# Mixture-of-experts stage: the order of 16 tiles of 512 rows and 7 of 256

## The chip, the cores and the metric

The kernel runs on one core of a Trainium2 chip. The core has five engines that run side by side, each with its own instruction stream: TensorE (PE, matmuls), VectorE (DVE), ScalarE (ACT), GpSimd (POOL) and SyncE (SP, which here only starts DMAs). They wait for each other through semaphores. The metric is the device time of one execution in microseconds; lower is better.

## What is computed

One decoder layer on x of shape 16 x 256 x 256 in float32: linear attention with decay, cross attention to a short context, and a mixture of 8 experts of which each token uses two, each stage followed by a residual and a layer norm. Only the last part matters here:

```python
probs = softmax(xf @ router_w.T); topv, topi = top_k(probs, 2)
mask = zeros.at[arange(n)[:, None], topi].set(1.0)
probs = probs * mask / (sum(probs * mask) + 1e-09)
g = einsum('nd,edf->nef', xf, gate_w) + gate_b     # d = 256, f = 512
u = einsum('nd,edf->nef', xf, up_w) + up_b
h = silu(g) * u
expert_out = einsum('nef,efd->ned', h, down_w) + down_b
y = einsum('ne,ned->nd', probs, expert_out)
x = layernorm(x + y)
```

4096 tokens with two experts each give 8192 rows of work.

## The kernel before

**Stages.** `linear_attention`, `cross_attention`, `route_tokens`, `run_experts` and `combine` run one after the other. The expert stage runs from about 1046 us to 1442 us of the span.

**Tiles.** `Plan` cuts the expert work into tiles. A tile belongs to one expert. There are BIGS = 16 tiles of T = 512 rows (four blocks of 128) and HALVES = 7 of HALF = 256 rows (two blocks), enough for every split of the rows over the experts. The big tiles are numbered 0 to 15 and the half ones 16 to 22. `blocks(t)` gives a tile's blocks and `first_block(t)` where its rows stand in the table of slots; `blocks_of_parity(t, turn)` and `rounds(t)` count blocks for the semaphores. `route_tokens` finds each row's slot and writes in `expert_of` and `tile_table` which expert each tile has.

**One tile.** Products of float32 are made from a high and a low part: hi x hi + hi x lo + lo x hi. In its turn for tile t each engine does the following, in the order of its code.

- PE: gate and up for f = 0, 1 (`gate_up`, L2095), the down product of tile t-1 block by block (`down`, L2107), the transposes of the rows of tile t+1 (`turn_x`, L2084), and gate and up for f = 2, 3. A big tile has 48 gate/up matmuls of 512 columns, a half one 48 of 256; a down has 12 matmuls of 256 columns per block. Two blocks of `down` fit in PSUM; the third waits until DVE has taken the first (`y_kept`).
- ACT: the high part of the gate/up weights of t+1 (`gu_high`, L1895), silu of gate 0 and 1 (L1917), the scaling of the y rows of t-1 by the router's share (L1927) between the high parts of h (L1923), the high part of the rows of t+1 (L1907), gates 2 and 3, and the high part of the down weights of t+1 (L1901).
- DVE: h for f = 0, 1 (L2023), then `keep_y` of t-1: a cast of the row numbers (`e_target<-e_token`, L1987, one column for each block) and one addition for each block that takes it out of PSUM (L1991). Then the low part of the rows of t+1 (L1980), the shares of t+1 (L2004), the row numbers to gather for t+2 (`e_index`, L2013), h and its low parts (L2029), and the low part of the down weights (L1996).
- POOL: the low part of the gate/up weights of t+1 (`low_parts`, L1862, four subtractions), `add_rows` of t-1 (L1873, one indirect DMA for each block that adds y rows to `sum_rows`), and `gather_rows` of t+2 (L1853, one indirect DMA for each block). The addition waits until ACT has scaled the rows (`y_scaled`).
- SP: the weights of t+2 (L1808 for gate and up, L1812 for down), 1.5 MB for a tile of either size, and the biases of t+1 after the y rows of t-1 are kept.

All buffers that depend on a tile are double, by the parity of t. `all_tiles` writes out tiles 0 and 1, runs tiles 2 to 13 in a hardware loop of two tiles an iteration, and writes out tiles 14 to 22.

## Time and profile before

| | |
|---|---|
| median of 3 runs | 1469.36 us (1468.21 to 1469.93) |
| the profiled execution | 1471.37 us, of it the span 1469.7 us |
| mean granted TensorE clock | 0.949 of full |
| busy: PE, PEld, DVE, ACT, POOL | 90%, 76%, 55%, 65%, 54% |
| six tiles 9 to 14 | 106.4 us |
| tile 15 | 23.1 us |
| tiles 16 to 21 | 76.9 us |
| tile 22, to the end of its tail | 14.4 us |

A tile is counted here from its first gate/up matmul. PE is TensorE's matmuls and PEld its weight loads, which overlap. In a timeline a row gives start, length, engine, line, operation, what is written and read, shapes and a count of merged instructions; brackets hold the idle time before it and what ended it. PEclk is the share of the full TensorE clock of 2.4 GHz that was granted, so 0.50 is 1.2 GHz. Matmuls overlap, so the length of one is more than the distance to the next.

### The profile page before, as it was taken

To read this page: it belongs to the slowest core of one execution; us is meant where nothing else is said; L and a number is where in the kernel's file an instruction comes from. 1 tells how busy PE (TensorE), PEld (TensorE's weight loads), DVE (VectorE), ACT (ScalarE), POOL (GpSimd) and SP (SyncE) were. 2 spreads that over 40 slices of the span, in tenths; PEclk is the share of its full clock that TensorE was granted. 3 is DMA by queue.
4 is the path that set the end of the run, shared out by engine and by line. 5 is a ranking of instruction groups with operands and counts; after the bars stand their busy time and mean duration, and the time that the engine had idled before them with its cause. 6 is when DMAs were issued, how large, how long until landed. Compare 5 with 4: busy or idle time off the path is not lost. (4 is left out here: it accounts for less than half of the span.)

```text
span 1469.7 us, 31082 instructions
## 1 busy us (share of the span) xinstructions
PE 1322.1 (90%) x10437; PEld 1120.0 (76%) x10437; DVE 811.3 (55%) x1684; ACT 953.2 (65%) x2168; POOL 796.1 (54%) x885
## 2 busy tenths in 40 slices
PE   5899999999999999999987999973599999998780
PEld 4788888888888888888775777752488888888780
DVE  4345554455554455554556888848355555555464
ACT  4677777777777777777754777763455655665453
POOL 2244444444444444444555777740468888886863
PEclk9999999999999999999998999985699999999895
DMA  3300100000000010000023444323346666665637
GB/s 136 81 11 27 31 23 30 16 28 25 30 23 30 15 30 24 31 30 23 23 65 91 113 111 111 98 74 92 105 109 151 154 151 154 168 156 122 193 77 236
DMA packets 136852, 117.55 MB, mean 80 GB/s; under 512 B 46578, under 2 KB 121690, under 8 KB 136730
## 3 DMA queue, kind: packets, MB, share of 16 engines
q1 hardware_dynamic: 121754, 95.36, 21.4%
q0 software_dynamic: 14976, 20.62, 7.8%
q8 instruction: 70, 1.15, 0.3%
q14 instruction: 52, 0.43, 0.1%
HBM read 79.89 MB, written 33.58 MB: 77 GB/s over the span
## 5 line engine op out<-in xcount | busy, mean ns | idle before, releaser
L345 POOL TENSOR_SCALAR_AFFINE_SELECT a_decay<-a_decay 128x256 f32<-128x256 f32 x256 | 115.2, 454 | 258.3 <-ACT a_decay L433 256.8
L565 DVE TENSOR_TENSOR a_probs<-a_ps_s,a_decay 128x384 f32<-128x384 f32 x256 | 131.6, 552 | 158.6 <-PE a_ps_o L752 147.5
L354 POOL TENSOR_TENSOR a_key_sum<-a_probs 128x256 f32<-128x256 f32 x128 | 94.5, 738 | 169.9 <-DVE a_probs L565 157.9
L396 ACT ACTIVATE a_qk_exp<-a_ps_qk 128x512 f32<-128x512 f32 x128 | 76.5, 598 | 137.5 <-PE a_ps_qk L658 130.0
L1873 POOL DMA_INDIRECT sum_rows<-e_y_out,e_target x78 | 124.4, 1594 | 48.2 <-ACT e_y_out L1927 21.1
L658 PE MATMUL a_ps_qk<-a_xT_hi,a_w_hi 128*128 128x256 f32 x512 | 144.8, 283 | 3.6 <-ACT a_qk_relu L397 3.6
L658 PE MATMUL a_ps_qk<-a_xT_hi,a_w_lo 128*128 128x256 f32 x512 | 143.9, 281 | 0.0
L658 PE MATMUL a_ps_qk<-a_xT_lo,a_w_hi 128*128 128x256 f32 x512 | 143.7, 281 | 0.0
L558 DVE SCALAR_TENSOR_TENSOR a_qk<-a_qk_exp,a_qk_relu 128x512 f32<-128x512 f32 x128 | 89.1, 696 | 94.5 <-ACT a_qk_relu L397 94.3
L733 PE MATMUL a_ps_s<-a_qk 64*128 64x256 f32 (+1 forms) x1024 | 132.2, 338 | 0.7 <-DVE a_probs L565 0.5
L431 ACT ACTIVATE a_decay<-a_ps_c,a_c_now 128x256 f32<-128x256 f32 x256 | 124.4, 486 | 2.0 <-PE a_ps_c L723 1.2
L1853 POOL DMA_INDIRECT e_x_in<-x_rows,e_index x78 | 78.6, 1007 | 75.4 <-DVE e_index L2013 52.2
L1862 POOL TENSOR_TENSOR e_gu_lo<-e_gu_raw,e_gu_hi 128x512 fp32r<-128x512 f32 x88 | 110.4, 1290 | 8.9 <-ACT e_gu_hi L1895 8.5
L746 PE MATMUL a_ps_o<-a_probs,a_values 128*64 128x256 f32 (+1 forms) x1024 | 111.5, 338 | 0.4 <-DVE a_probs L565 0.4
L733 PEld LDWEIGHTS a_ps_s<-a_qk 64*128 64x128 f32 x1024 | 107.8, 187 | 2.5 <-issue 2.5
L658 PEld LDWEIGHTS a_ps_qk<-a_xT_hi,a_w_hi 128*128 128x128 f32 x512 | 97.8, 191 | 5.7 <-issue 5.6
L2107 PE MATMUL e_ps_y<-e_dn_hi,e_hid_hi 128*128 128x256 f32 x312 | 91.0, 292 | 9.4 <-DVE e_y_out L1991 7.3
L433 ACT ACTIVATE a_decay<-a_ps_c,a_c_now 128x128 f32<-128x128 f32 x256 | 98.4, 385 | 0.0
L658 PEld LDWEIGHTS a_ps_qk<-a_xT_hi,a_w_lo 128*128 128x128 f32 x512 | 98.0, 191 | 0.0
L658 PEld LDWEIGHTS a_ps_qk<-a_xT_lo,a_w_hi 128*128 128x128 f32 x512 | 97.8, 191 | 0.0
L359 POOL TENSOR_TENSOR a_oT_lo<-a_oT,a_oT_hi 128x256 fp32r<-128x256 f32 x128 | 94.3, 737 | 1.2 <-ACT a_oT_hi L450 1.2
L1033 POOL TENSOR_TENSOR b_probs<-b_probs,b_top 128x1232 f32<-128x1232 f32 x32 | 72.8, 2274 | 40.8 <-DVE b_top L1228 40.8
(317 smaller groups left out, 4008.1 us busy)
## 6 DMA issues: line engine op xcount, KB each, us to landing
e_gu_raw<-in_L_ffn_gate_w SPq DMA_DIRECT2D x23, 512.0 KB
e_gu_raw<-in_L_ffn_up_w SPq DMA_DIRECT2D x23, 512.0 KB
e_dn_raw<-in_L_ffn_down_w SPq DMA_DIRECT2D x23, 512.0 KB
a_x_in<-in_x SPq DMA_DIRECT2D x16, 256.0 KB, 2.7
a_x_res<-in_x SPq DMA_DIRECT2D x16, 256.0 KB
x_rows<-a_x SPq DMA_DIRECT2D x16, 256.0 KB, 2.2
x_bo_rows<-a_x_bo SPq DMA_DIRECT2D x16, 256.0 KB, 2.2
b_x_bo<-x_bo_rows SPq DMA_DIRECT2D x16, 256.0 KB, 2.8
```

The lines of the kernel that those rows point to most:

```text
L345: pool.affine_select(out=d, in_=d, compare_op=ALU.is_ge, fill=0.0, base=0, pattern=[[0, 2], [1, P]], channel_multiplier=-1)\
L354: pool.tensor_tensor(key_sum[:], probs[:, :, P:N], probs[:, :, N:TRI], ALU.add).then_inc(keys_summed, 1)
L359: pool.tensor_tensor(oT_lo[g % 2][:], oT[g % 2][:], oT_hi[g % 2][:].bitcast(F32), ALU.subtract).then_inc(oT_lo_done, 1)
L431: act.activation(decay[h][:, 0:N], ps_c[:, h, :], ACT.Exp, bias=c_now[:, 0, head:head + 1], scale=-1.0)
L433: act.activation(decay[h][:, N:TRI], ps_c[:, h, P:N], ACT.Exp, bias=c_now[:, 1, head:head + 1], scale=-1.0).then_inc(decay_exp[h], 1)
L565: vec.tensor_tensor(probs[:, h, :], ps_s[h][:, 0:TRI], decay[h][:], ALU.mult)\
L658: mm = pe.matmul(out, l, r, start=(n == 0), stop=(n == len(todo) - 1))
L733: mm = pe.matmul(ps_s[h][:, out], qk[g][rows, 1, j], qk[g][rows, 0, i], start=True, stop=True)
L746: pe.matmul(out[h][:, 0, cols], values[par][:, j, 2 * g + h, :], probs[:, h, keys], start=(j == 0), stop=(j == 1), skip_group_check=True)
L1862: ins = pool.tensor_tensor(gu_lo[par][:, k, cols], gu_raw[par][:, k, cols], gu_hi[par][:, k, cols].bitcast(F32), ALU.subtract)
L1873: pool.indirect_dma_start(sum_dram, bass.IndirectOffsetOnAxis(target[par][:, blk:blk + 1], 0), y_out[par][:, blk, :], None, compute_op=ALU ...
L2107: mm = pe.matmul(ps_y[n][:, 0:D], h[:, f, rows], w[par][:, f, :], start=(s == 0), stop=(s == len(todo) - 1))
```

## The change

The same 16 big and 7 half tiles run in another order. With ALONE = BIGS - HALVES = 9, tiles 0 to 8 are big; then come seven pairs of a big and a half tile: 9, 11, ..., 21 are big and 10, 12, ..., 22 are half. The slots in the table stay where they were (big ones first), so `first_block` jumps, and a new `blocks_done` counts the blocks of all tiles ahead for the semaphores. The loop now covers tiles 2 to 5, and tiles 6 to 22 are written out. `route_tokens` numbers the tiles in the new order with an iota of two dimensions and makes three comparisons where there were two.

```diff
+        self.ALONE = self.BIGS - self.HALVES
+        assert self.TOKENS <= 4096 and self.ALONE >= 4
...
+    def is_half(self, t):
+
+        return isinstance(t, int) and t > self.ALONE and (t - self.ALONE) % 2 == 1
+
     def blocks(self, t):
 
-        return (self.T if not isinstance(t, int) or t < self.BIGS else self.HALF) // P
+        return (self.HALF if self.is_half(t) else self.T) // P
+
+    def blocks_done(self, t):
+
+        return sum(self.blocks(n) for n in range(t)) if isinstance(t, int) else t * (self.T // P)
 
     def first_block(self, t):
 
-        if not isinstance(t, int) or t <= self.BIGS:
+        if not isinstance(t, int) or t <= self.ALONE:
             return t * (self.T // P)
-        return (self.BIGS * self.T + (t - self.BIGS) * self.HALF) // P
+        pair = (t - self.ALONE) // 2
+        if self.is_half(t):
+            return (self.BIGS * self.T + pair * self.HALF) // P
+        return (self.ALONE + pair) * (self.T // P)
...
-            for n, tiles in enumerate((slice(0, BIGS), slice(BIGS, TILES))):
-                wide = [P, tiles.stop - tiles.start, E - 1]
+            for n, tiles in ((0, slice(0, ALONE)), (0, slice(ALONE, TILES, 2)), (1, slice(ALONE + 1, TILES, 2))):
+                wide = [P, len(range(TILES)[tiles]), E - 1]
...
-            with eng.Fori(1, (BIGS - 2) // 2) as i:
+            looped = (plan.ALONE - 2) // 2
+            with eng.Fori(1, looped) as i:
...
-            for t in range(BIGS - 2, TILES):
+            for t in range(2 * looped, TILES):
                 tile(t, t % 2, t // 2)
...
-                pool.wait_ge(y_scaled, first_block(t + 1))
+                pool.wait_ge(y_scaled, blocks_done(t + 1))
```

Two places show what moves. POOL, before, from tile 14 to tile 17; in each tile the low parts of the next one's weights, the additions of the last one's rows, the gathers for the next but one:

```order
L1862 TENSOR_TENSOR e_gu_lo1<-e_gu_raw1,e_gu_hi1 128x512 x4
L1873 DMA sum_rows<-e_y_out1,e_target1 4608x256 x4
L1853 DMA e_x_in0<-x2_rows,e_index0 128x260 x2
L1862 TENSOR_TENSOR e_gu_lo0<-e_gu_raw0,e_gu_hi0 128x512 x4
L1873 DMA sum_rows<-e_y_out0,e_target0 4608x256 x4
L1853 DMA e_x_in1<-x2_rows,e_index1 128x260 x2
L1862 TENSOR_TENSOR e_gu_lo1<-e_gu_raw1,e_gu_hi1 128x512 x4
L1873 DMA sum_rows<-e_y_out1,e_target1 4608x256 x4
L1853 DMA e_x_in0<-x2_rows,e_index0 128x260 x2
L1862 TENSOR_TENSOR e_gu_lo0<-e_gu_raw0,e_gu_hi0 128x512 x4
L1873 DMA sum_rows<-e_y_out0,e_target0 4608x256 x2
L1853 DMA e_x_in1<-x2_rows,e_index1 128x260 x2
```

POOL, the changed kernel, from tile 8 to tile 11 (the same code is at L1876, L1887 and L1867):

```order
L1876 TENSOR_TENSOR e_gu_lo1<-e_gu_raw1,e_gu_hi1 128x512 x4
L1887 DMA sum_rows<-e_y_out1,e_target1 4608x256 x4
L1867 DMA e_x_in0<-x2_rows,e_index0 128x260 x2
L1876 TENSOR_TENSOR e_gu_lo0<-e_gu_raw0,e_gu_hi0 128x512 x4
L1887 DMA sum_rows<-e_y_out0,e_target0 4608x256 x4
L1867 DMA e_x_in1<-x2_rows,e_index1 128x260 x4
L1876 TENSOR_TENSOR e_gu_lo1<-e_gu_raw1,e_gu_hi1 128x512 x4
L1887 DMA sum_rows<-e_y_out1,e_target1 4608x256 x4
L1867 DMA e_x_in0<-x2_rows,e_index0 128x260 x2
L1876 TENSOR_TENSOR e_gu_lo0<-e_gu_raw0,e_gu_hi0 128x512 x4
L1887 DMA sum_rows<-e_y_out0,e_target0 4608x256 x2
L1867 DMA e_x_in1<-x2_rows,e_index1 128x260 x4
```

In a half tile (the third group) POOL adds four blocks and gathers two; in the big tile behind it, it adds two and gathers four. Before, a half tile in the middle of its row adds two and gathers two.

DVE, before, from the end of tile 17 into tile 18, both half:

```order
L1996 TENSOR_TENSOR e_dn_lo<-e_dn_raw,e_dn_hi 128x1024
L2023 SCALAR_TENSOR_TENSOR e_hid<-e_ps_u,e_bias,e_gate 128x256 x2
L1987 CAST e_target<-e_token 128x2
L1991 TENSOR_TENSOR e_y_out<-e_ps_y,e_dn_bias 128x256 x2
L1980 TENSOR_TENSOR e_xT_lo<-e_ps_x,e_xT_hi 128x256 x2
```

DVE, the changed kernel, from the end of a big tile into the half tile behind it:

```order
L2010 TENSOR_TENSOR e_dn_lo<-e_dn_raw,e_dn_hi 128x1024
L2037 SCALAR_TENSOR_TENSOR e_hid<-e_ps_u,e_bias,e_gate 128x256 x2
L2001 CAST e_target<-e_token 128x4
L2005 TENSOR_TENSOR e_y_out<-e_ps_y,e_dn_bias 128x256 x4
L1994 TENSOR_TENSOR e_xT_lo<-e_ps_x,e_xT_hi 128x512 x2
```

In a half tile the cast now has four columns and is followed by four additions, in every one of the seven; before, in one.

## Rows read from the trace of the kernel before

**Rows 1.** The page, part 1: busy us (share of the span) and instructions of each engine.

```profile
PE 1322.1 (90%) x10437; PEld 1120.0 (76%) x10437; DVE 811.3 (55%) x1684; ACT 953.2 (65%) x2168; POOL 796.1 (54%) x885
```

**Rows 2.** Stretches: tiles 9-14, 15, 16-21, 22; first row names the columns.

```profile
core 0: us, PE busy (x) PEld busy (x) DVE busy (x) ACT busy (x) POOL busy (x), PEclk, DMA share, GB/s
1211.70:1318.10 106.40, 105.77 (x626) 93.97 (x625) 60.18 (x115) 63.59 (x96) 91.59 (x72) 1.00 0.63 156
1318.10:1341.20 23.10, 19.81 (x101) 17.68 (x101) 13.77 (x20) 10.04 (x16) 13.12 (x11) 0.85 0.46 109
1341.20:1418.10 76.90, 62.99 (x481) 61.29 (x480) 40.98 (x103) 45.33 (x86) 65.41 (x52) 0.93 0.62 160
1418.10:1432.50 14.40, 11.95 (x96) 11.59 (x96) 8.07 (x20) 5.94 (x14) 5.98 (x4) 1.00 0.34 38
```

**Rows 3.** Timeline of PE: start, length, line, operation; brackets: idle before, releaser.

```profile
1329.91 0.58 PE L2107 MATMUL e_ps_y<-e_dn_hi,e_hid_hi 128*128 128x256 f32 x1 [3.29 <-DVE e_y_out L1991]
...
1335.20 0.70 PE L2084 MATMUL e_ps_x<-ident,e_x_in 128*128 128x128 f32 x4
...
1341.22 0.28 PE L2095 MATMUL e_ps_g<-e_xT_hi,e_gu_hi 128*128 128x256 f32 x1
...
1351.91 0.66 PE L2084 MATMUL e_ps_x<-ident,e_x_in 128*128 128x128 f32 x4 [1.39 <-DMA e_x_in<-x_rows,e_index]
...
1366.73 1.11 PE L2084 MATMUL e_ps_x<-ident,e_x_in 128*128 128x128 f32 x4 [5.46 <-DMA e_x_in<-x_rows,e_index]
...
1374.31 0.28 PE L2107 MATMUL e_ps_y<-e_dn_hi,e_hid_hi 128*128 128x256 f32 x1
...
1391.38 1.12 PE L2084 MATMUL e_ps_x<-ident,e_x_in 128*128 128x128 f32 x4 [4.29 <-DMA e_x_in<-x_rows,e_index]
...
1400.06 0.28 PE L2107 MATMUL e_ps_y<-e_dn_hi,e_hid_hi 128*128 128x256 f32 x1
...
1414.01 0.66 PE L2084 MATMUL e_ps_x<-ident,e_x_in 128*128 128x128 f32 x4 [1.26 <-DMA e_x_in<-x_rows,e_index]
...
1431.97 0.28 PE L2107 MATMUL e_ps_y<-e_dn_hi,e_hid_lo 128*128 128x256 f32 x1
```

**Rows 4.** Timeline of DVE: the casts of row numbers, and a y row kept.

```profile
1072.02 3.05 DVE L1987 CAST e_target<-e_token 128x4 uint32<-128x4 f32 x1
...
1307.62 0.16 DVE L1987 CAST e_target<-e_token 128x4 uint32<-128x4 f32 x1
...
1325.17 4.35 DVE L1987 CAST e_target<-e_token 128x4 uint32<-128x4 f32 x1
...
1346.55 0.16 DVE L1987 CAST e_target<-e_token 128x4 uint32<-128x4 f32 x1
...
1350.56 0.42 DVE L1991 TENSOR_TENSOR e_y_out<-e_ps_y,e_dn_bias 128x256 f32<-128x256 f32 x1 [1.01 <-PE e_ps_y L2107]
...
1376.16 0.31 DVE L1987 CAST e_target<-e_token 128x2 uint32<-128x2 f32 x1
```

**Rows 5.** Timeline of POOL: low parts, additions and gathers.

```profile
1309.49 5.03 POOL L1862 TENSOR_TENSOR e_gu_lo<-e_gu_raw,e_gu_hi 128x512 fp32r<-128x512 f32 x4
...
1324.52 4.97 POOL L1862 TENSOR_TENSOR e_gu_lo<-e_gu_raw,e_gu_hi 128x512 fp32r<-128x512 f32 x4
1337.91 1.62 POOL L1873 DMA_INDIRECT sum_rows<-e_y_out,e_target  x1 [8.42 <-ACT e_y_out L1927]
...
1345.39 1.01 POOL L1853 DMA_INDIRECT e_x_in<-x_rows,e_index  x1 [0.31 <-ACT e_gu_hi L1895]
...
1347.71 5.00 POOL L1862 TENSOR_TENSOR e_gu_lo<-e_gu_raw,e_gu_hi 128x512 fp32r<-128x512 f32 x4
...
1361.87 0.98 POOL L1853 DMA_INDIRECT e_x_in<-x_rows,e_index  x1 [0.30 <-issue]
...
1411.34 0.98 POOL L1853 DMA_INDIRECT e_x_in<-x_rows,e_index  x1 [0.31 <-issue]
```

**Rows 6.** Timelines of ACT (high part of weights) and SP (weights issued).

```profile
1343.46 1.90 ACT L1895 CAST e_gu_hi<-e_gu_raw 128x2048 fp32r<-128x2048 f32 x1
...
1356.05 0.40 SPq L1808 DMA_DIRECT2D e_gu_raw<-in_L_ffn_gate_w  x1
```

More of the change, by code:

```diff
@@ L1475, in __init__ @@
         self.COLS = self.ROWS // P
-        assert self.TOKENS <= 4096 and self.BIGS % 2 == 0
+        self.ALONE = self.BIGS - self.HALVES
+        assert self.TOKENS <= 4096 and self.ALONE >= 4
     def halves_needed(self, experts):
@@ L1488, in halves_needed @@
         return worst
+    def is_half(self, t):
+        return isinstance(t, int) and t > self.ALONE and (t - self.ALONE) % 2 == 1
     def blocks(self, t):
-        return (self.T if not isinstance(t, int) or t < self.BIGS else self.HALF) // P
+        return (self.HALF if self.is_half(t) else self.T) // P
+    def blocks_done(self, t):
+        return sum(self.blocks(n) for n in range(t)) if isinstance(t, int) else t * (self.T // P)
     def first_block(self, t):
-        if not isinstance(t, int) or t <= self.BIGS:
+        if not isinstance(t, int) or t <= self.ALONE:
             return t * (self.T // P)
-        return (self.BIGS * self.T + (t - self.BIGS) * self.HALF) // P
+        pair = (t - self.ALONE) // 2
+        if self.is_half(t):
+            return (self.BIGS * self.T + pair * self.HALF) // P
+        return (self.ALONE + pair) * (self.T // P)
     def blocks_of_parity(self, t, turn):
-        if not isinstance(t, int) or t < self.BIGS:
+        if not isinstance(t, int):
             return self.T // P * (turn + 1)
-        return (self.BIGS // 2 * self.T + (turn + 1 - self.BIGS // 2) * self.HALF) // P
+        return sum(self.blocks(n) for n in range(t % 2, t + 1, 2))
 def route_tokens(nc, sh, plan, logits, slot_col, slot_row, counts, x2_dram, expert_of, tile_table):
     E, D = sh.E, sh.D
-    NBK, T, HALF, BIGS, TILES = plan.BLOCKS, plan.T, plan.HALF, plan.BIGS, plan.TILES
+    NBK, T, HALF, BIGS, TILES, ALONE = plan.BLOCKS, plan.T, plan.HALF, plan.BIGS, plan.TILES, plan.ALONE
     with ExitStack() as ctx:
@@ L1566, in _ @@
             pool.iota(order_i[:], pattern=[[-1, E]], base=E, channel_multiplier=0).then_inc(consts_step, 1)
-            pool.iota(tile_no_i[:, 0:BIGS], pattern=[[1, BIGS]], base=0, channel_multiplier=0).then_inc(consts_step, 1)
-            pool.iota(tile_no_i[:, BIGS:TILES], pattern=[[1, TILES - BIGS]], base=0, channel_multiplier=0).then_inc(consts_step, 1)
+            pool.iota(tile_no_i[:, 0:ALONE], pattern=[[1, ALONE]], base=0, channel_multiplier=0).then_inc(consts_step, 1)
+            pool.iota(tile_no_i[:, ALONE:TILES].rearrange("p (n k) -> p k n", k=2), pattern=[[-ALONE, 2], [1, TILES - BIGS]],
+                      base=ALONE, channel_multiplier=0).then_inc(consts_step, 1)
             pool.iota(count_i[:], pattern=[[1, P]], base=0, channel_multiplier=0).then_inc(consts_step, 1)
@@ L1711, in run_experts @@
     T, BIGS, TILES = plan.T, plan.BIGS, plan.TILES
-    blocks, first_block = plan.blocks, plan.first_block
+    blocks, first_block, blocks_done = plan.blocks, plan.first_block, plan.blocks_done
     TB, FC = T // P, FF // P
@@ L2001, in shares @@
                 if has(t, -2):
-                    vec.wait_ge(y_scaled, first_block(t - 1))
+                    vec.wait_ge(y_scaled, blocks_done(t - 1))
                 nb = blocks(t)
```

2 lines of the change are left out of this document (1 added, 1 removed).

## The prediction

> **What bounds the kernel now.** I read the page first: TensorE is busy for 90% of the span [rows 1]. That average hides the stage the change touches, so next I cut the expert stage into stretches [rows 2]. Six 512-row tiles (9 to 14) take 106.4 us, 17.7 each, with PE busy 105.8 of them at the full clock: PE bounds them. Tile 15, also of 512 rows, takes 23.1. The six 256-row tiles 16 to 21 take 76.9, so 12.8 each, and the last one 14.4 up to the end of its tail. Then the PE timeline [rows 3], for what a wait costs. Last the timelines of DVE, POOL and of ACT and SP [rows 4 to 6], for what PE waited for.
>
> PE's own work, from the spacing of its matmuls (0.228 us for 512 columns, 0.12 for 256): a big tile without waits is 17.5 us (gate and up 2 x 5.5, down 5.75, transposes 0.8), a half tile 9.1 (2 x 2.95, 2.9, 0.4). So a half tile loses 3.7 us and a big one 0.2. Two things take the time.
>
> First, **the loop of the rows**. In tile t POOL does the low parts of the weights of t+1 (5.2 us: 5.0 and a gap), adds the rows of t-1 to DRAM (7.5 for four blocks, 1337.91 to 1345.39, so 3.8 for two), and gathers the rows of t+2 (2.3 for two, up to 1347.71, so 4.9 for four with the gap) [rows 5]. Half tile: 11.3 on POOL against 9.1 on PE. PE waited for gathered rows 1.39, 5.46, 4.29 and 1.26 us [rows 3]. A gather that ends while weights are in flight lands late: the one of tile 18 left POOL at 1362.85 [rows 5], weights had been issued from 1356.05 on [rows 6], and PE restarted at 1366.73, 3.9 later. Where no weights move it is nearer 1.7 (1414.01, with POOL done at 1412.32).
>
> Second, **a stall of DVE behind POOL**. In tile t DVE casts the row numbers of tile t-1 (e_target) just before it empties the first down result. With POOL elsewhere that takes 0.16 us; the two four-column casts that began inside POOL's low parts took 3.05 and 4.35, each up to the end of the last of the four subtractions (1325.17 + 4.35 = 1329.52; 1324.52 + 4.97 = 1329.49) [rows 4, 5]. PE waited 3.29 us for it, ran the rest of down in 5.3 in place of 2.9 (1329.91 to 1335.20, at half clock for most of it), and POOL's add, which needs these rows, started 2.7 after that, having been idle 8.42 [rows 3, 5]. That is the 23.1 of tile 15. It happened there because tile 14 gathers two blocks and not four, so POOL began the low parts 2.6 us sooner: 0.65 before the cast, while in tile 14 they began 1.87 after it (1307.62, 1309.49). The two-column casts that began inside the low parts (two of them, 0.31 and 0.30) lost only 0.15.
>
> **The change part by part.** *Instructions:* the same 23 tiles, 16 of four blocks and 7 of two, the same weights loaded 23 times. Matmuls, casts and DMAs neither grow nor shrink: 0. Routing gets one more small DVE compare of about 0.2 us in a serial chain: +0.2. Five more pairs of tiles are written out in place of the loop; tiles 14 and 15 were so already, and 14 ran at 17.6: 0, at most a few tenths. *Tiles 0 to 8* are as before: 0.
>
> *Tile 9* now gathers as before's tile 15 did: tile 8 gathers two blocks, so the low parts start early under a four-column cast. It costs 23.1 again, but in place of tile 15, not on top. From here I use the clock of before, in which the changed kernel is 106.4 ahead: tile 9 runs 1318.1 to 1341.2.
>
> *Tile 10 (half):* POOL starts gathering tile 11 at 1345.39, now four blocks: 1350.2. PE ends down of tile 9 at 1350.3. Rows land 1.7 to 4.2 later; with 2.7, transposes and second gate/up half done at 1358.0 (some of it at low clock). *Tile 11 (big):* 5.5 + 2.9 to 1366.4. POOL: low 5.2, add 7.5, two gathers 2.3, so 1365.25; rows at 1368.2; 0.4 + 5.5: tile 12 begins at 1374.1. Tiles 10 and 11 take 32.9, 2.4 over the 30.5 of one half and one big tile of before.
>
> *Tile 12 (half), where the sum is decided.* After its gather (1365.25) POOL needs 5.2 + 3.8 + 4.9 = 13.9 and could begin the low parts of tile 13 at 1379.15, 5.0 us into tile 12. They can't start before ACT's high part, which ends 4.1 into such a tile (tile 16 began at 1341.22; 1343.46 + 1.90) [rows 3, 6]. DVE's cast comes at 5.3 (1346.55 - 1341.22) [rows 4]. In tile 16 of before the low parts came at 6.5, since POOL was late; here they come between 4.3 and 5.0, ahead of the cast, and the cast is of a big tile: four columns. So it stalls to the end of the low parts.
>
> One pair from there, half tile first, beginning at 0: low parts 4.3 to 9.35; PE has stood since 5.9, restarts at 9.75 (0.4 after the low parts, as at 1329.49 to 1329.91), two slow blocks 5.3: 15.05. Transposes 0.8, gate/up 2.95: big tile begins at 18.8. 5.5 + 2.9: 27.2. POOL: add at 15.05 + 2.7 = 17.75, plus four adds and two gathers 9.8 (1337.91 to 1347.71): 27.55. Weights are issued some 5 us after DVE has the last y row (1350.98, then 1356.05) [rows 4, 6], so at 20 to 21, and the gather ends 6.5 behind them, as for tile 18 (1356.05 to 1362.85): rows 4.2 later, 31.8. A wait of 4.6. Then transposes 0.8, gate/up 5.5, and 1.6 for the low clock (after 5.46 and 4.29 of waiting, transposes and 48 half-width matmuls took 7.6 and 8.7 us against 6.3, so 1.3 and 2.4): 39.6 [rows 3]. POOL could begin the next low parts at 27.55 + 13.9 = 41.45, 1.9 into the next half tile; ACT holds them to 4.3. The stall repeats: it feeds itself.
>
> Sum: tile 12 at 1374.1; five pairs (12 to 21) of 39.6 = 198.0; tile 22 has no low parts beside it, so no stall: before 13.9 from 1418.1 to the last matmul at 1432.0, plus 2.9 for a down of four blocks = 16.8. End of PE at 1588.9 - 106.4 = 1482.5 against 1432.0: **+50.5**, and 0.2 for routing. The profiled execution took 1471.4, so 1522; the median of the runs is 2.0 under it: **1520**. *Bounds of a pair:* 38.0 if no clock is lost at the second wait, 41 if both waits lose 2.4. If tile 12 just escapes (its margin is 0.3 to 1 us) one pair is cheaper by 7.
>
> The Trainium skill, page "SBUF — State Buffer", section "Who interferes with whom", says that a cast in a two-port mode and a GpSimd instruction take a shared port pair, and that whoever comes first keeps it for its whole instruction. The trace agrees that the cast is blocked, but 4.35 us is four subtractions, not one (about 1.3). By one instruction the cast would get in after the first subtraction; that is rival A.
>
> **Rivals.** *A, the cast gets in between two subtractions* and loses under 1.3 us. For it: the two-column casts began 1.0 us into the low parts, as the cast of tile 12 will, and lost 0.15; the two long ones began 0.6 before a boundary, so it may hang on timing and not on width. Against: those two passed two and three boundaries. A pair then: down done at 8.7 to 9.4, POOL adds at 11.4, gather done 21.2, rows 3 to 4 us later, 24.9 (PE ready at 20.8), 0.4 + 5.5 + 0 to 2: 31 to 33, against 30.5 for one big and one half tile of before (17.7 + 12.8). Five of 32 and the rest as above: 1374.1 + 160 + 16.8 - 106.4 = 1444.5, so **+12.5**, 1482.
>
> *B, faster: POOL runs back to back.* If the rows land in 1.7 us (no weights in flight at the second gather) and no cast is caught, half tile and big tile share POOL's load: 15.0 + 13.9 = 28.9 a pair, under the 30.5 of before. Then low parts come 6.2 into the half tile, past the cast at 5.3, and the state holds itself. 1374.1 + 144.5 + 16.8 - 106.4 = 1429.0: **-3**, 1466. If tiles 9 to 11 went better too, -10. It decides at a landing of 2.6 us: 13.9 - 5.9 - landing must exceed 5.3. Against it: the weights go out about 6.5 before that gather ends, and such gathers landed after 3.9 to 4.3.
>
> *C, the order doesn't matter:* equal work gives equal time, 1467 to 1472, if gains of B and losses of A cancel, or the pattern alternates.
>
> **How the numbers follow.** The forecast 0.54 (1505 to 1530); A, and mixtures of it with the forecast, 0.28 (1476 to 1505); C 0.06; B 0.12. The range takes in the forecast, A and the upper half of C: 1470 to 1530. A measurement can tell 0.2% (3 us) from no change. Faster is B, 0.12; same is C, 0.06; slower is the forecast and A, 0.82.
>
> **What would show it.** In the profile after: e_target casts of four columns of 3 us and more in tiles 12, 14, 16, 18 and 20, each ending with the low parts; PE waits of about 4 us for e_y_out and then 4 to 5 us for e_x_in in each pair; a pair of 39 to 40; mean PE clock in that stretch clearly under 0.93; POOL idle before its adds by 8 us in each half tile. Casts of 0.2 to 1.3 and pairs of 32 would be A. Low parts later than 5.3 us into the half tiles and pairs under 30 would be B, and then the term that failed is the landing of the gathers. Tiles 0 to 8 should end at the same time within a microsecond; if not, the written-out tiles or the routing cost what I set at 0.

## The result, and the profile after

The changed kernel takes 1495.6 us (median; 1492.38 to 1504.84) against 1468.8 for the kernel before, measured beside it: a ratio of 1.0194, with a 95% interval of 1.0174 to 1.0214. It is slower, as forecast, and inside the range of 1470 to 1530, but by 27 us and not by 50.

The profiled execution took 1492.38 (span 1490.7), 21.0 more than the one of before. I cut it where the matmuls show the tiles: tile 9 begins at 1210.96, tile 12 at 1267.53, tile 22 at 1431.37, and the last matmul starts at 1449.72. Windows of the changed kernel: tiles 9 to 11, the five pairs 12 to 21, tile 22.

```profile
core 0: us, PE busy (x) PEld busy (x) DVE busy (x) ACT busy (x) POOL busy (x), PEclk, DMA share, GB/s
1210.96:1267.53 56.57, 48.13 (x282) 43.02 (x280) 34.18 (x55) 27.34 (x46) 40.76 (x32) 0.94 0.54 136
1267.53:1431.37 163.84, 142.58 (x901) 127.86 (x901) 101.79 (x180) 89.32 (x151) 130.44 (x100) 0.97 0.56 144
1431.37:1449.72 18.35, 16.17 (x120) 15.83 (x120) 9.78 (x21) 7.29 (x16) 5.96 (x5) 0.91 0.23 28
```

Tile 12 begins where the prediction had it (1374.1 - 106.4 = 1267.7). Then it parts from it: five pairs take 163.8 us, 32.8 each, not 39.6. What PE waited for in them (each line gives the total, how often, and the longest; the longest wait for e_hid, 2.0, is the one just ahead of tile 22):

```profile
engine line waited for: us in total, times, longest us
PE e_ps_x L2098 <- DMA e_x_in<-x_rows,e_index: 15.3, 7, 3.8
PE e_ps_g L2109 <- DVE e_hid L2037: 7.5, 8, 2.0
```

Not one wait of PE for e_y_out is left there, the wait on which the forecast rested. The DVE timeline shows why. These are casts of e_target, to be read against [rows 4]: tile 9, tile 11, tile 14 (half), tile 15, tile 21.

```profile
1217.99 4.42 DVE L2001 CAST e_target<-e_token 128x4 uint32<-128x4 f32 x1
...
1257.28 5.32 DVE L2001 CAST e_target<-e_token 128x2 uint32<-128x2 f32 x1
...
1307.83 0.27 DVE L2001 CAST e_target<-e_token 128x4 uint32<-128x4 f32 x1
...
1323.39 5.26 DVE L2001 CAST e_target<-e_token 128x2 uint32<-128x2 f32 x1
...
1421.38 5.16 DVE L2001 CAST e_target<-e_token 128x2 uint32<-128x2 f32 x1
```

The four-column casts in the half tiles took 0.16 to 0.27. The two-column ones, in the big tiles 11, 15, 17, 19 and 21, took 5.2 to 5.4 us: the stall was there, but in the big tiles. Tile 13 alone escaped (0.16): its cast began 0.84 ahead of POOL's low parts, those of the others 0.13 to 0.45. In a big tile the down product is that of a half one, two blocks, and both fit in PSUM. So PE was not held there by the stall; it waited later, for e_hid. POOL, from tile 13 into tile 16 of the changed kernel (to be read against [rows 5]):

```profile
1303.74 0.95 POOL L1867 DMA_INDIRECT e_x_in<-x_rows,e_index  x1 [0.30 <-issue]
1306.78 5.06 POOL L1876 TENSOR_TENSOR e_gu_lo<-e_gu_raw,e_gu_hi 128x512 fp32r<-128x512 f32 x4 [2.09 <-ACT e_gu_hi L1909]
1313.84 1.62 POOL L1887 DMA_INDIRECT sum_rows<-e_y_out,e_target  x1 [2.00 <-ACT e_y_out L1941]
...
1322.67 0.98 POOL L1867 DMA_INDIRECT e_x_in<-x_rows,e_index  x1 [0.30 <-issue]
1323.68 4.94 POOL L1876 TENSOR_TENSOR e_gu_lo<-e_gu_raw,e_gu_hi 128x512 fp32r<-128x512 f32 x4
1331.89 1.62 POOL L1887 DMA_INDIRECT sum_rows<-e_y_out,e_target  x1 [3.27 <-ACT e_y_out L1941]
```

In the big tile POOL goes from its gather, which ends at 1323.65, straight into the four subtractions. The cast had begun 0.29 before them and ended with them (1323.39 + 5.26 = 1328.65; 1323.68 + 4.94 = 1328.62). The y rows came late, POOL's addition waited 3.27 for them, and so POOL was late in the next half tile. Its low parts began 7.8, 4.3, 6.4, 6.3 and 7.8 us into the half tiles, in four of five after DVE's cast at 5.3 to 5.7. The one at 4.3 is tile 14, the only one with no stall in the big tile ahead of it. So a stall in a big tile kept the low parts of the next half tile off the cast. It is not why tile 14 had no stall: there the cast did begin inside the low parts, and took 0.27.

The additions at the end, POOL in the changed kernel:

```profile
1444.75 1.65 POOL L1887 DMA_INDIRECT sum_rows<-e_y_out,e_target  x1 [11.47 <-issue]
...
1455.02 1.54 POOL L1887 DMA_INDIRECT sum_rows<-e_y_out,e_target  x1 [3.06 <-DMA sum_rows<-e_y_out,e_target]
1456.87 1.56 POOL L1887 DMA_INDIRECT sum_rows<-e_y_out,e_target  x1 [0.30 <-issue]
```

And the last three in the kernel before:

```profile
1427.99 1.75 POOL L1873 DMA_INDIRECT sum_rows<-e_y_out,e_target  x1 [0.30 <-issue]
1434.07 1.54 POOL L1873 DMA_INDIRECT sum_rows<-e_y_out,e_target  x1 [4.33 <-ACT e_y_out L1971]
1435.92 1.54 POOL L1873 DMA_INDIRECT sum_rows<-e_y_out,e_target  x1 [0.30 <-issue]
```

Tile 21 is a big one now, so four additions stand ahead of the last two, and those wait 3.06 for them to land. From the start of the last matmul to the start of the last addition it is 7.2 us (1449.72 to 1456.87), before it was 3.9 (1431.97 to 1435.92). So the 21.0 are 17.7 up to the last matmul and 3.3 behind it. Of the 17.7, 1.1 came before the stage of the experts; its start moves from 1048.3 to 1053.4 between the profiled executions of all the kernels here, whose code ahead of it differs in the routing alone, so I give that to no cause. Tiles 0 to 8 took 158.9 against 160.9 before, where PE waited five times for e_y_out, 2.0 in tile 1 and 0.3 to 0.4 in four others; in the changed kernel only the 2.0 is left. So from tile 9 on the changed kernel lost 18.6: the six pairs of tiles 10 to 21 cost 14.9 more than tiles 9 to 14 and 16 to 21 of before, six big and six half as well (198.2 against 183.2), tile 22 cost 4.5 more (18.35 against 13.86), and tile 9 0.8 less than tile 15 of before.

### The profile page after: what moved, and what is told of

The parts are those of the page before. It is cut to its first block and busy times, and to the rows that moved or that the text cites. A ratio compares the mean times of both kernels' runs of the same rounds, so it can differ in the third digit from the quotient of the medians.

```text
span 1490.7 us, 30839 instructions
## 1 busy us (share of the span) xinstructions
PE 1328.2 (89%) x10437; PEld 1122.5 (75%) x10437; DVE 834.7 (56%) x1685; ACT 952.9 (64%) x2168; POOL 799.1 (54%) x885
## 3 DMA queue, kind: packets, MB, share of 16 engines
q1 hardware_dynamic: 121754, 95.36, 21.1%
## 5 line engine op out<-in xcount | busy, mean ns | idle before, releaser
L1887 POOL DMA_INDIRECT sum_rows<-e_y_out,e_target x78 | 124.8, 1600 | 66.8 <-ACT e_y_out L1941 33.3
L1867 POOL DMA_INDIRECT e_x_in<-x_rows,e_index x78 | 81.4, 1043 | 75.7 <-DVE e_index L2027 52.5
L1876 POOL TENSOR_TENSOR e_gu_lo<-e_gu_raw,e_gu_hi 128x512 fp32r<-128x512 f32 x88 | 110.2, 1287 | 6.6 <-ACT e_gu_hi L1909 6.1
```

Of the source, the lines that this page charges most:

```text
L1876: ins = pool.tensor_tensor(gu_lo[par][:, k, cols], gu_raw[par][:, k, cols], gu_hi[par][:, k, cols].bitcast(F32), ALU.subtract)
L1887: pool.indirect_dma_start(sum_dram, bass.IndirectOffsetOnAxis(target[par][:, blk:blk + 1], 0), y_out[par][:, blk, :], None, compute_op=ALU ...
```

## The experiments

Two theories at first. **S:** stalled casts make the pairs long. **L:** the loop of the rows does, with gathers that land late behind the weights, and the stalls lie in its shadow. Later a third: **P**, POOL's own work bounds a pair (28.9).

**Casts on ACT, in the changed kernel and in the one before.** The same edit in both; nothing else moves.

```diff
 def scale_y(blk):        # ACT
...
     for blk in range(blocks(t - 1) - 1):
         scale_y(blk)
+        if blk == 0:
+            act.copy(target[1 - par][:, 0:blocks(t - 1)], token[...]).then_inc(target_ready, 1)
...
 def keep_y(t, par, turn):        # DVE
-    vec.tensor_copy(target[par][:, 0:blocks(t)], token[...]).then_inc(target_ready, 1)
```

> The changed kernel with one edit: the cast of the row numbers (e_target) is made by ACT, behind its first scaling, and no longer by DVE, so nothing of DVE's can stand behind POOL's low parts there. Theory S (the casts that stand behind POOL's low parts cost the time): the stalls of tiles 1 and 9 give back 3.7 and 5.9 us, and those of tiles 11, 15, 17, 19 and 21 the 3.3 us by which POOL's additions were late, so the pairs fall from 32.8 to 29 to 30 and the time from 1495.6 to 1465 to 1475. Theory L (the landing of the gathered rows sets the pairs, the stalls are hidden behind it): only tiles 1 and 9 gain, pairs stay at 32 to 33, time 1484 to 1488.

Measured: 1480.03 (1474.92 to 1481.83), ratio to before 1.0071 (1.0046 to 1.0095). No cast is left to stall, and 15.6 us are gone; but pairs still take 32.6 (162.80 / 5, window below). The gain is in tile 1 (21.28 to 17.53), tile 9 (22.24 to 17.12), and 0.6 to 1.2 each in tiles 10, 11 and 22. Most of the saving lies outside the pairs, which speaks for L there.

```profile
1256.47:1419.27 162.80, 145.98 (x902) 130.87 (x900) 81.95 (x170) 90.67 (x160) 127.48 (x101) 0.94 0.58 145
```

> The kernel before with the same edit (e_target cast by ACT). Both theories: tiles 1 and 15 lose their stalls, 3.7 and 5.9 us less, so about 1459; the half tiles 16 to 21 stay at 12 to 13 us each, since no cast of theirs was long. What it decides is whether the new order is faster or slower than the old one where neither has stalls: by S the changed kernel with this edit is within 10 us of this one, by L it is 25 us behind.

Measured: 1461.46 (1459.83 to 1461.83), ratio 0.9952 (0.9936 to 0.9969): tile 1 falls to 17.5 and tile 15 from 23.1 to 17.1. With no stalled cast in either, the new order is still 18.6 us slower than the old one. By this pair of runs the stalls, on which the forecast rested, are not the main loss. How much of the 18.6 is the clock is read further down.

**Light weights, in the changed kernel.**

```diff
-load_gate_up(e, par)
+load_gate_up(e, par, 32)      # columns loaded of each 512
...
-load_down(e, par)
+load_down(e, par, 32)         # columns loaded of 256
```

> The changed kernel in which the weights of tiles 2 to 22 are loaded only in part (32 of 512 columns of gate and up, 32 of 256 of down), so that the gathers meet nearly no weights in flight; the output is therefore not the reference's. Theory S: the casts still stand behind the low parts, POOL's additions are still late by 3.3 us, pairs stay at 31 to 33 us, time 1488 to 1496. Theory L: the rows land some 1.7 us after POOL is done in place of 3.4 to 4.2, pairs fall to about 30, time 1478 to 1484.

Measured: 1480.01 (a single execution). Pairs fell to 31.1, with the stalls still there in tiles 9, 11, 15 and 19 (4.35 to 5.60 us), and PE's waits for rows in the pairs from 15.3 to 7.2 us. The time is L's number. The pairs are not: 31.1 is above L's 30 and at the edge of S's 31 to 33, so the landing is a part of the loss and not all.

**The cast a microsecond later, in the changed kernel**, to see whether its moment decides.

```diff
 if has(t, -1):
+    if isinstance(t, int) and t > plan.ALONE and not plan.is_half(t):
+        vec.tensor_reduce(idle[:], count[:].unsqueeze(1).to_broadcast([P, 7, P]), AX.X, ALU.max)
     keep_y(t - 1, 1 - par, turn - 1 + par)
```

> The changed kernel with an idle reduction of about 1 us on DVE ahead of the cast in the big tiles 11 to 21 (nothing else changes), so that the cast begins about 1 us after POOL's low parts have begun and not around their start. If it is the moment that decides (casts that began 1.0 us into the low parts lost 0.15, those up to 0.73 in waited for the end of all four), the long casts of tiles 11, 15, 17, 19 and 21 shrink to 0.2 to 0.4 us and the time falls by some 5 to 10 us. If what decides is that POOL came to the low parts straight from its gathers, without an idle stretch before, they still last to the end of the low parts, about 4 us each, and the time stays or grows by a few us.

Measured: 1494.09 (a single execution), as the changed kernel. Here are the casts of tile 14 (half) and tile 15 (big), and POOL's low parts in the same two tiles:

```profile
1308.38 0.32 DVE L2002 CAST e_target<-e_token 128x4 uint32<-128x4 f32 x1
...
1325.01 4.18 DVE L2002 CAST e_target<-e_token 128x2 uint32<-128x2 f32 x1
```

```profile
1307.37 5.04 POOL L1877 TENSOR_TENSOR e_gu_lo<-e_gu_raw,e_gu_hi 128x512 fp32r<-128x512 f32 x4 [0.45 <-ACT e_gu_hi L1910]
...
1324.19 4.96 POOL L1877 TENSOR_TENSOR e_gu_lo<-e_gu_raw,e_gu_hi 128x512 fp32r<-128x512 f32 x4
```

Both casts begin inside the low parts, 1.00 and 0.82 us in. One takes 0.32 and the other 4.18, to the end of the fourth subtraction. Two others in that kernel, in tiles 19 and 21, began 0.98 and 1.00 in and took 4.04 each. So the width of the cast does not decide: four columns were held in tile 9 and not in tile 14.

The moment is not ruled out, close as these are. Four casts that began inside the low parts got through in all the traces: tile 14 here and in the changed kernel, and tiles 18 and 20 of the kernel before. Each began 0.25 to 0.29 us ahead of the end of the first subtraction and ended 0.02 to 0.03 behind it. So they did get in between two subtractions. The first subtraction of tile 14 in the changed kernel ends at 1308.08, its cast, shown above, at 1308.10:

```profile
1306.78 1.30 POOL L1876 TENSOR_TENSOR e_gu_lo<-e_gu_raw,e_gu_hi 128x512 fp32r<-128x512 f32 x1 [2.09 <-ACT e_gu_hi L1909]
```

In tile 20 of the kernel before it ends at 1402.11, and the cast at 1402.13:

```profile
1400.81 1.30 POOL L1862 TENSOR_TENSOR e_gu_lo<-e_gu_raw,e_gu_hi 128x512 fp32r<-128x512 f32 x1 [2.93 <-ACT e_gu_hi L1895]
...
1401.83 0.30 DVE L1987 CAST e_target<-e_token 128x2 uint32<-128x2 f32 x1
```

The held casts that began inside a subtraction did so 0.31 us or more ahead of its end, and the edit brought none nearer. Two more things part the groups. POOL came to the held ones' subtractions without a pause, and to the others' only after it had waited 0.45 to 2.93 for ACT. And the held ones stood in tiles of odd number, always big, the others in even, half ones, so they also write the other of the two `target` buffers. These coincide in every case, and no run here tells which of them matters for the cast.

**The cast early on DVE, in the changed kernel:** at the start of DVE's work of a tile.

```diff
+if has(t, -1):
+    target_rows(t - 1, 1 - par, turn - 1 + par)   # the wait for y_stored and the cast
 hidden(0)
 hidden(1)
```

> The changed kernel with the cast still on DVE, but at the start of DVE's work of a tile and not ahead of the first down result: in a big tile some 5 to 7 us sooner. If the loss comes from the moment (POOL going from its gathers straight into four subtractions around +7.3), the casts take 0.16 to 0.3 us in the big tiles, and pairs are as with ACT's cast, 32 to 33: 1478 to 1488. If a gather itself holds the cast (POOL is in additions and gathers until +7.3), casts take 1 to 2 us each wherever they meet one. If the cast is held whenever POOL is anywhere in its run from additions to low parts: over 5 us, and the time is over 1500.

Measured: 1469.71 (a single execution). Every cast took 0.15 to 0.17, although in the big tiles it stood among POOL's additions. In tile 11 it lies wholly inside one:

```profile
1240.93 0.16 DVE L2001 CAST e_target<-e_token 128x2 uint32<-128x2 f32 x1
```

```profile
1239.72 1.59 POOL L1887 DMA_INDIRECT sum_rows<-e_y_out,e_target  x1 [0.30 <-issue]
```

This addition didn't hold it. That it came out 10 us under the version with ACT's cast was in no expectation. In the pairs its waits for rows are about as long (12.0 and 12.5 in all); the clock is what differs there, 7.1 of 7.6 us. Of the rest of the 10, its expert stage began 2.4 sooner. Against the old order without stalls (1461.46) the new one is then 8.3 behind and not 18.6, by this one execution: a good part of the 18.6 was the clock. Tile 17 of the version with ACT's cast, and its first transpose:

```profile
1335.86:1356.35 20.49, 17.15 (x76) 14.39 (x77) 8.26 (x18) 9.08 (x16) 17.56 (x15) 0.83 0.81 193
```

```profile
1347.75 0.47 PE L2106 MATMUL e_ps_x<-ident,e_x_in 128*128 128x128 f32 x1 [3.34 <-DMA e_x_in<-x_rows,e_index]
```

Tile 17 of the version with the early cast:

```profile
1331.04:1348.37 17.33, 14.53 (x76) 12.41 (x77) 8.22 (x19) 9.01 (x15) 15.31 (x12) 1.00 0.76 184
```

```profile
1342.40 0.66 PE L2103 MATMUL e_ps_x<-ident,e_x_in 128*128 128x128 f32 x4 [2.80 <-DMA e_x_in<-x_rows,e_index]
```

This gives the pieces of a pair. In these two versions a big tile less its wait for rows is 14.5 or 14.6 with a clock of 1.00 (17.33 - 2.80, 17.07 - 2.52, 17.73 - 3.16), 16.1 or 16.2 at 0.91 and 17.2 to 17.4 at 0.83. A half tile without a stall is 13.77. So a pair has a floor of 28.3, and the five pairs of every version come out as a sum (us; waits and clock read for each big tile; the rest is what is left over, so it holds what stalls and DVE add, and the lower clock, 0.88 or 0.89, of half tile 12 in the changed kernel and of 12 and 16 with light weights):

| version of the changed kernel | five pairs | floor | PE's wait for rows in big tiles | low clock, big tiles | rest |
|---|---|---|---|---|---|
| as changed | 163.8 | 141.6 | 13.3 | 3.2 | 5.7 |
| light weights | 155.7 | 141.6 | 7.2 | 0 | 6.9 |
| ACT's cast for the pairs only | 160.1 | 141.6 | 14.7 | 3.2 | 0.6 |
| ACT's cast | 162.8 | 141.6 | 12.5 | 8.7 | 0 |
| early cast | 155.2 | 141.6 | 12.0 | 1.6 | 0 |
| ACT's cast, light weights | 146.5 | 141.6 | 4.9 | 0 | 0 |
| ACT's cast, gather sooner | 150.3 | 141.6 | 4.7 | 0 | 4.0 |
| that, and DVE helps POOL | 148.0 | 141.6 | 2.8 | 0 | 3.6 |

By this sum the stalls cost 5.7 to 6.9 in five pairs: 2.1 in a big tile where no wait for rows covers them (tile 21: 17.13 - 0.45 = 16.7 against 14.55), and up to 1.9 in the half tile behind, most of that a wait for rows there (1.69 in tile 20). Where the stalls were taken away with the weights whole, more waiting (14.7 against 13.3) or a lower clock (8.7 against 3.2) took their place in two versions of three.

**ACT's cast for the pairs only** (for the rows of tiles 11 to 22), the direct trial of S against L.

```diff
 def keep_y(t, par, turn):
-    vec.tensor_copy(target[par][...], token[...]).then_inc(target_ready, 1)
+    if not (isinstance(t, int) and t >= 11):
+        vec.tensor_copy(target[par][...], token[...]).then_inc(target_ready, 1)
```

> The changed kernel; ACT casts the row numbers for tiles 11 to 22, DVE still those of tiles 0 to 10. So the stalls of tiles 1 and 9 stay and only those of the pairs go (tiles 11, 15, 17, 19, 21). Theory S (a stalled cast is what makes a pair long): each of the five costs PE its own wait and slow down blocks, 2 to 3.5 us, so 10 to 15 less than the changed kernel: 1481 to 1486. Theory L (the loop of the rows makes the pair long: a gather that lands 3.3 to 4.2 us late, in both halves of a pair, and the stalls lie in its shadow): pairs stay at 32.6 against 32.8 and the time falls by 1 to 4 only, 1491 to 1495. The rest of what was won when ACT made every cast (15.6 us) then came from tiles 1 and 9 to 12.

Measured: 1486.15 (1484.43 to 1489.55), ratio 1.0115 (1.0093 to 1.0136). The cast of tile 10's rows, which DVE makes in tile 11, stayed on DVE and was held for 5.17 us, so four of the five stalls are gone. That is 9.5 under the changed kernel by medians, at the edge of what S said; the two profiled executions lie only 2.9 apart in span, and the pairs 3.8. The changed kernel's own runs spread over 12 us, and the table shows one thing that can do it: the clock after a wait. So the stalls of the pairs cost 3 to 10 us: by the profiled executions what L allowed (1 to 4), by the medians just short of S (10 to 15). This run alone does not choose between them.

**ACT's cast and light weights:** neither stall nor late landing.

> Leaves out part of the computation: the weights of tiles 2 to 22 are loaded only in part (32 of 512 columns of gate and up, 32 of 256 of down), everything else runs; and ACT casts the row numbers in every tile. So neither a stall nor a congested landing of gathers is left. If what remains of a pair is POOL's own work back to back (theory P: 15.0 + 13.9 = 28.9 in the prediction): pairs of 28.9 to 29.5, five pairs 15 to 18 us less than the 32.6 of the version with the weights whole, last matmul at 1417 to 1421, time 1458 to 1464. If light weights alone (pairs 31.1, stalls left in) had already taken all that the landing costs, pairs stay at 30.5 to 31 and the time is 1467 to 1471. If PE bounds a pair (17.5 + 9.1 = 26.6) it is under 1452.

Measured: 1458.19 (a single execution). Pairs of 29.3, at a clock of 1.00. POOL runs from one big tile's low parts to the next (tiles 15 and 17) in 29.2 us with no pause but the 0.2 to 0.3 around its DMAs:

```profile
1251.91:1398.41 146.50, 137.21 (x902) 124.41 (x900) 85.62 (x170) 90.39 (x160) 129.36 (x101) 1.00 0.44 72
```

```profile
1302.50 5.01 POOL L1876 TENSOR_TENSOR e_gu_lo<-e_gu_raw,e_gu_hi 128x512 fp32r<-128x512 f32 x4
1307.68 1.62 POOL L1887 DMA_INDIRECT sum_rows<-e_y_out,e_target  x1 [0.17 <-issue]
...
1315.73 0.95 POOL L1867 DMA_INDIRECT e_x_in<-x_rows,e_index  x1 [0.30 <-issue]
1316.70 5.04 POOL L1876 TENSOR_TENSOR e_gu_lo<-e_gu_raw,e_gu_hi 128x512 fp32r<-128x512 f32 x4
...
1331.69 1.29 POOL L1876 TENSOR_TENSOR e_gu_lo<-e_gu_raw,e_gu_hi 128x512 fp32r<-128x512 f32 x1
```

P's number, and the pattern of rival B: with weights in flight for a short time only, POOL back to back, and it holds itself. Of the 21.8 us between this and the version with whole weights, 16.3 are in the pairs: 7.6 of waits for rows and 8.7 of clock.

**The gather sooner, in the changed kernel with ACT's cast:** POOL issues it between the two halves of its additions, from tile 9 on.

```diff
-add_rows(t - 1, 1 - par, turn - 1 + par)
-gather_rows(t + 2, par, turn + 1)
+first = blocks(t - 1) // 2
+add_rows(t - 1, 1 - par, turn - 1 + par, range(first))
+gather_rows(t + 2, par, turn + 1)
+add_blocks(t - 1, 1 - par, range(first, blocks(t - 1)))
```

> The changed kernel with the casts on ACT, and in tiles 9 to 20 POOL issues its gather after the first half of the additions in place of after all of them, then the second half. Same work on every engine. Theory L: in a half tile the gather of the next half tile's rows leaves POOL two additions (3.7 us) sooner, in a big tile one addition (1.9) sooner, so PE's wait for e_x_in (2.7 to 3.3 us a tile, and the low clock behind it) mostly goes: pairs of 29 to 30 in place of 32.6, 1462 to 1468. Rival P: POOL is busy through the pair anyway and the additions that now come last delay its next low parts: pairs 31.5 to 32.6, 1474 to 1480. Rival: the gather sooner needs the buffer sooner (POOL waits for the transposes of the tile or for the row numbers): no gain either, and a wait of POOL ahead of the gather shows it.

Measured: 1465.52 (1464.28 to 1467.6), ratio 0.9979 (0.9969 to 0.9989). Pairs of 30.1, and PE's waits for rows fell from 12.5 to 6.0 with the same work on every engine and the weights whole:

```profile
PE e_ps_x L2106 <- DMA e_x_in<-x_rows,e_index: 12.5, 5, 3.3
```

```profile
PE e_ps_x L2115 <- DMA e_x_in<-x_rows,e_index: 6.0, 7, 1.6
```

The first line is of ACT's cast alone, the second of this version. In tile 15 the last gather leaves POOL 5.6 us into the tile and not 7.4, and PE gets the rows 4.2 to 4.3 behind its end in both (tile 15 began at 1302.91 with ACT's cast alone):

```profile
1309.34 0.98 POOL L1867 DMA_INDIRECT e_x_in<-x_rows,e_index  x1 [0.31 <-issue]
```

```profile
1314.48 0.33 PE L2106 MATMUL e_ps_x<-ident,e_x_in 128*128 128x128 f32 x1 [2.99 <-DMA e_x_in<-x_rows,e_index]
```

and in this version, where it began at 1298.31:

```profile
1302.88 0.98 POOL L1867 DMA_INDIRECT e_x_in<-x_rows,e_index  x1 [0.30 <-issue]
```

```profile
1308.18 0.55 PE L2115 MATMUL e_ps_x<-ident,e_x_in 128*128 128x128 f32 x3 [1.30 <-DMA e_x_in<-x_rows,e_index]
```

The wait shrank by about what the gather gained (1.7 of 1.9), and no tile of the five pairs lost its clock any more. That settles where most of the excess of ACT's cast alone was: of 21.2 over the floor 7.8 of waiting and 8.7 of clock went, and a rest of 4.0 came in. What stands beside that rest is another operation of DVE that is held, the first of `shares`, which takes 0.21 to 0.25 in tiles 13 to 19 with ACT's cast alone. Here POOL's low parts come later in the big tiles, and in the five of tiles 13 to 21 it took 2.2 to 2.9, to the end of the low parts, ahead of the next e_hid. In tile 15:

```profile
1307.13 5.57 POOL L1876 TENSOR_TENSOR e_gu_lo<-e_gu_raw,e_gu_hi 128x512 fp32r<-128x512 f32 x4
...
1310.23 2.50 DVE L2035 SCALAR_TENSOR_TENSOR e_share<-e_x_in,expert_of 128x2 f32<-128x2 f32 x1
```

No run takes this stall away alone, so how much of the 4.0 it is stays open. The same edit **in the kernel before** (ACT's cast, from tile 15 on):

> The kernel before with the casts on ACT, and in tiles 15 to 20 POOL issues its gathers after the first half of the additions. With ACT's cast alone tiles 16 to 21 took 77.5 us (14.5, 17.1, 9.6, 15.2, 9.8, 11.3) with 13.3 of PE waits for gathered rows. If the landing of gathers makes the long half tiles long too, as it did in the pairs (32.6 to 30.1 by the same edit), they fall towards POOL's 11.3 each: 68 to 72, so 5 to 9 less than 1461.5: 1452 to 1457. Rival: one addition (1.9 us) sooner is too little, or POOL's low parts come later by as much and delay the weights: 1459 to 1463.

Measured: 1459.8 (1459.19 to 1460.85), ratio 0.9935 (0.9915 to 0.9954). The main line of the forecast missed, 1.7 us instead of 5 to 9; its rival had 1459 to 1463. Half tiles 16 to 21 took 77.1 us against 77.5. The last gather ahead of tile 17's long wait, and the wait, in the kernel before with ACT's cast:

```profile
1348.57 0.98 POOL L1853 DMA_INDIRECT e_x_in<-x_rows,e_index  x1 [0.30 <-issue]
```

```profile
1353.65 0.69 PE L2092 MATMUL e_ps_x<-ident,e_x_in 128*128 128x128 f32 x2 [5.53 <-DMA e_x_in<-x_rows,e_index]
```

and with the gather sooner:

```profile
1347.08 0.98 POOL L1853 DMA_INDIRECT e_x_in<-x_rows,e_index  x1 [0.30 <-issue]
```

```profile
1354.16 0.69 PE L2101 MATMUL e_ps_x<-ident,e_x_in 128*128 128x128 f32 x2 [5.66 <-DMA e_x_in<-x_rows,e_index]
```

From the end of the gather on POOL to PE it is 4.1 us in the one (1349.55 to 1353.65) and 6.1 in the other (1348.06 to 1354.16). SP had issued gate, up and down weights from 1342.50 and from 1344.05 on. The gather left POOL 1.5 sooner, the gate and up weights left SP 1.6 later, and the rows came 0.5 later. In tile 19 the gather left 0.6 sooner, gate and up went out at the same time, the down weights 0.9 later, and the rows came 0.8 later. So the rows did not follow their own instruction here. That they followed the weights is a reading of these two tiles, and no run moved the weights alone.

This trace also has a case for the open point above. In its tile 18, a half one of even number, the first operation of `shares` began 0.25 ahead of the end of the third subtraction (1367.51) and was held past it, to the end of the fourth. POOL had come to these subtractions without a pause:

```profile
1363.16 5.58 POOL L1862 TENSOR_TENSOR e_gu_lo<-e_gu_raw,e_gu_hi 128x512 fp32r<-128x512 f32 x4
...
1367.26 1.51 DVE L2021 SCALAR_TENSOR_TENSOR e_share<-e_x_in,expert_of 128x2 f32<-128x2 f32 x1
```

That speaks for POOL's pause and against the moment and the number of the tile, but it is one case, and of another operation.

**DVE makes the fourth subtraction.** In the kernel before with ACT's cast:

```diff
 def low_parts(par, turn):        # POOL: three of four
-    for k in range(KC):
-        for cols in (slice(0, FF), slice(FF, 2 * FF)):
+    for k, cols in ((0, slice(0, FF)), (0, slice(FF, 2 * FF)), (1, slice(0, FF))):
...
+vec.tensor_tensor(gu_lo[1 - par][:, 1, FF:2 * FF], gu_raw[...], gu_hi[...], ALU.subtract)   # DVE, behind tile_index
```

> The kernel before with the casts on ACT, and DVE makes the fourth of the four low-part subtractions of each tile from the second on (POOL three): 1.25 us less of POOL's work a tile. Where the half tiles are bound by POOL's loop (11.3 us of POOL against 9.1 of PE in six of them, and they take 12.8 in the kernel before) each gets 0.5 to 1.2 us shorter: 3 to 7 us less than with ACT's cast alone (1461.5), so 1454 to 1458. Rival: DVE's subtraction meets POOL's on the shared path and stalls DVE or is late for PE's first product with the low part, as the casts were: no gain or a loss, 1461 to 1475, with PE waits for e_gu_lo from DVE.

Measured: 1460.34 (1459.82 to 1461.9), ratio 0.9949 (0.9933 to 0.9965): no gain that can be told. All three edits together, in the kernel before and in the changed one:

> The kernel before with all three edits: casts on ACT, gathers between the halves of the additions from tile 15 on, DVE makes one of the four subtractions. The last edit alone gave 1.1 us (1461.5 to 1460.3), since the gathers' landing stood in front of it. If the two limits are the landing and POOL's sum, each edit pays more once the other is there: half tiles of 10 to 11, 60 to 66 for tiles 16 to 21, 1446 to 1453. If DVE's subtraction only moves work from POOL to a DVE that is late anyway: as without it, 1452 to 1460.

> The changed kernel with the same three edits (gathers between the halves of the additions from tile 9 on). With two of them its pairs took 30.1 us, POOL's own work in a pair being 28.9. DVE's part takes 2.5 of that: 26.4, and PE's own is 26.6. If POOL is what bounds a pair now: 27.5 to 29 a pair, 5 to 12 less, 1453 to 1460. If the landing still does: 29.5 to 30, 1463 to 1466. In either case the order of before, with the same edits, should stay ahead by the first half tiles' cheaper rows or by the tail (3 us).

Measured: in the kernel before 1457.94 (1456.57 to 1459.36), ratio 0.9927 (0.9906 to 0.9947), tiles 16 to 21 in 75.1; in the changed one 1461.7 (1459.9 to 1462.99), ratio 0.9946 (0.9925 to 0.9968), pairs of 29.6. The forecasts' main lines (1446 to 1453, 1453 to 1460) were too low, and their rivals (1452 to 1460, 1463 to 1466) held or nearly so. In the changed kernel POOL's work shrank by 2.5 a pair, but DVE's grew. Against ACT's cast alone PE's wait for e_hid at the start of each big tile went from 0.74 to 1.4, and the half tile ahead of it, which contains that wait, from 13.77 to 14.43. In the kernel before, half tiles 17 and 19 still waited 4.7 and 4.1 for rows.

```profile
1328.22 0.47 PE L2132 MATMUL e_ps_g<-e_xT_hi,e_gu_hi 128*128 128x512 f32 x1 [1.39 <-DVE e_hid L2054]
```

The best version found is the old order with all three edits, 10.8 us under the kernel before. With the same edits the new order is never ahead: 18.6 behind with the cast on ACT, 5.7 with the gather sooner too, 3.8 with all three.

## Why the prediction was partly right

- **Where the time was to be lost: right.** Tile 9 took 22.2 (forecast 23.1) and its cast 4.42. Tile 12 began 0.2 us from its forecast place, in part by luck: tile 9 began 0.7 early and was 0.9 shorter than forecast, and tiles 10 and 11 were 1.4 longer (34.3 against 32.9).
- **Landing of gathers: right.** From POOL's gather to PE's restart: 4.5, 4.6, 4.0 and 3.8 us in tiles 13, 15, 17 and 19, forecast 4.2. In tile 21 it was 1.8, and PE waited 0.45 there. The late landing held rival B off; light weights together with ACT's cast let it in.
- **"The two-column casts ... lost only 0.15": the step that failed.** It took from two casts of the kernel before, in half tiles 18 and 20 (the first is in [rows 4], the second is shown above), that a narrow cast is safe anywhere. In five big tiles such casts lost 5 us each. I had the timing of the big tiles in the working (POOL back to back through them) and did not ask whether DVE's cast meets the low parts there.
- **The stall of the half tiles: did not come.** Low parts were forecast between 4.3 and 5.0. In tiles 12, 16, 18 and 20 they came at 6.3 to 7.8, POOL having been held up by the stall in the big tile ahead, which I had left out. In tile 14 they came at 4.32, as forecast, and the cast inside them still took 0.27: the step from "inside the low parts, four columns" to "held to their end" failed there too. With no stalled cast at all (ACT's cast) they do come at 4.33, in tiles 14, 16, 18 and 20, as worked out. Whether a cast there would be held is then the open point above; tile 14 says no. The term "pair 39.6" was 34.2 too large over five; 0.4 of each pair was a slip of the sum, which took the transposes of a big tile's rows (0.8) where PE turns those of a half tile (0.4). That the measured time lies in the range is owed to rival A's part of it, and to rows that landed late as forecast, not to the stalls that were forecast.
- **Rival A** gave 31 to 33 a pair and +12.5. The pairs measured 32.8, the stage +17.7. Its size was right by luck, and its mechanism in one tile of five: in tile 14 the cast did get in after the first subtraction, ending 0.02 behind it, and in the other four half tiles it never met the low parts. The pair was as long as A had it through waits for rows, which A had, and through stalls in the big tiles, which it had not. The Trainium skill, page "SBUF — State Buffer", section "Who interferes with whom", has the loser blocked for the whole instruction of the other; the traces agree for the four casts that got through after one subtraction, and show more for the held ones: four instructions in a row, 5.3 us.
- **PE's own floor of a pair** was set at 26.6 and is 28.3: 0.74 of the 1.7 is a wait for e_hid ahead of each big tile, and some 0.4 a gap in the half tile's gate and up; the rest I can't place.
- **Clock.** 1.6 us for a low clock in each pair was the term; it came in two big tiles of five (13 and 17). In the other versions it is 0, 1.6 or 2.6 to 2.9 by tile.
- **Tile 22 and the tail.** 16.8 forecast, 18.35 measured at a clock of 0.91, behind a wait of 1.99 for e_hid after the stall of tile 21; with ACT's cast it took 17.19 at 1.00; and the four additions ahead of the last two, 3.3 us, were overlooked. The sum: 50.5 - 34.2 + 1.5 + 3.3 is 21.1, against 21.0 between the profiled executions. That it closes so well is luck too: the later start of the stage, the faster tiles 0 to 8, the shorter tile 9 and the longer tiles 10 and 11 are not in it, and cancel to 0.2. The medians stand 26.8 apart, since the profiled execution of the changed kernel was its fastest; which of its terms grows in the others I have no trace of.

## What to carry to other kernels

When a stall is found at one place of an order, look at every place of the new order where the same two engines meet, the one with the smaller operand too; a stall also delays the engine that waits for it, and so moves the place where the two meet next. Where an engine issues both gathers that the next stage waits for and additions that nobody does, let the gathers go first: half the additions behind them was worth 14.5 us, 12.5 of it in the pairs and more than half of that a clock that stayed up. It was worth 1.7 where the rows did not come sooner for it, so look at the time from issue to use before and after. Alternating large and small tiles costs the fixed parts of both (floor 28.3 against 27.1, which is 17.5 and 9.6, the shortest big and half tile in a row of their own kind), and a large tile next to last lengthens the tail.
